# A new hand-written order for the last three units, gates and experts, and a 128-column last tile in the value product

## The chip, the core and the metric

The program runs on one core of one Trainium2 chip. Its engines work side by side and meet only at semaphores: TensorE (PE in the rows; its weight loads are PEld), VectorE (DVE), ScalarE (ACT), GpSimd (POOL) and SyncE (SP), whose queue issues nearly all transfers. The metric is the time of one execution on the device in microseconds. The kernel before took 1152.41 us, the median of three runs (1150.47 to 1155.04).

## What is computed

Two layers over x of shape (2, 1024, 256), all in float32:

```python
x = _layernorm(x + _L0_attn_ref(x, qkv, o_proj, gamma, beta))        # one head of 256, causal
x = _layernorm(x + _L0_ffn_ref(x, wq, ..., be2))
# _L0_ffn_ref:
a = _attention(_layernorm(h0, ln1_w, ln1_b), wq, bq, wk, bk, wv, bv, wo, bo)   # 16 heads of 128, rope, causal
h = h0 + a
m = _moe(_layernorm(h, ln2_w, ln2_b), w_gate, we1, be1, we2, be2)   # 4 experts of 256, the best 2 weighted
return h + m
```

Inside a head, `scores = q @ k.T`, the causal mask, a softmax over keys, `out = probs @ v`, and `out @ wo`. The mask makes every tile above the diagonal zero.

## The kernel before, in words

The attention is cut into 34 *units*, numbered by `u`: units 0 and 1 are the first layer's two batches, units 2 to 33 are the 16 heads times two batches of the second layer (`LAST` is 33). A unit has 1024 rows, eight tiles of 128 (`i`), in two chunks of 512 (`c`).

Every product is done as three matmuls, since each operand is kept as a high part and a low part in a reduced float type (`_hi`, `_lo`): high times high, high times low, low times high. That is the helper `product` (line 424 in every row). The engines share one head like this:

- PE: `project_q(u, x)` (q or k of a chunk, six matmuls 512 wide), `project_v`, `scores(u, i)`, `transposes(u, i)` of the probabilities, `outputs(u, c)` (the value product), `out_project(u, c, g)`.
- ACT: `add_bias`, `exponent`, and the high parts: `high_qk`, `high_p`, `high_o`.
- DVE: `row_max` (mask and maximum), `rotate` (the cosine term of rope), the low parts `low_p`, `low_o`, and `accumulate` into `acc`.
- POOL: `turn` (the sine term of rope) and `low_qk`, the low part of q and k.
- SP: `swap`, which brings the halves of q or k to the other partitions for `turn`, and the loads.

`outputs(u, c)` accumulates over key tiles `j` into one bank of `ps_m`. For the four tiles on the diagonal it writes only the columns from `off` on:

```python
off = min(max(0, j - TC * c), 2) * P
...
last = product(out[:, off:CH], (v_hi[:, s, j, vals], v_lo[:, s, j, vals]),
               (pT_hi[:, slot, off:CH], pT_lo[:, slot, off:CH]), j == 0, j == tiles - 1)
```

So these four tiles are 512, 384, 256 and again 256 columns wide, where the last needs only 128. The 128 columns too many read zeros that POOL writes into slot 7 of `pT_hi` and `pT_lo` once, at the start.

The order of the work is written out by hand, for each engine apart, as a list of calls: `start()` for the first units, `head(u)` for units 3 to 30, and `ends()` for what is left. Nothing reorders it: an instruction that waits for its semaphore holds up all behind it on its engine. Two rules set the waits that the change touches. PE takes the two banks of `ps_m` in turn: `take_bank` waits until the reader of the bank's last but one use is done. And the transposes use the two banks of `ps_t` in turn, freed by `low_p`.

After unit 33, `ends()` runs the gates (`gate_logits`, then `gate_copy`, `gating_1` to `gating_3` on DVE) and the experts of both batches: `expert_in(b, n)`, `gelu_mid` and `high_mid` (in `middle`) on ACT, `low_mid` on POOL, `expert_out(b, n)`, and `mix_bias` and `mix` on DVE. `low_expert(m, e)` on POOL splits the expert weights, which `load_expert` brings through two staging slots; `ln_stats`, `ln_power`, `ln_apply`, `ln_transpose`, `ln_affine` and `ln_low` are the steps of a layer norm; `add_row` and `add_x1` are additions into `acc` on POOL.

Of the kernel before, what the change touches and what calls it, by code (L numbers as in the profile page):

```python
# [101 lines left out]
def build(nc, A):  # L102

    with ExitStack() as ctx:
# [2369 lines left out]
```

## Time and profile before

| | |
|---|---|
| median of three runs | 1152.41 us |
| the profiled execution | 1155.01 us, of it 1152.9 us span |
| PE / PEld busy | 1121.9 us (97%) / 1021.8 us (89%) |
| DVE / ACT / POOL busy | 866.1 (75%) / 736.6 (64%) / 637.8 (55%) |
| chain that ended last | PE 91%, DVE 5%, POOL 1%, ACT 1% |

The span runs from the first to the last instruction; the 2.1 us around it belong to the execution and not to the program. A busy PE is not a PE at its peak: a matmul is shown from its start to its modelled end, and the next one starts before that end. So the spacing of starts says what a matmul costs. "PEclk" is the granted clock of TensorE as a share of its higher level, 2.4 GHz; 0.50 is the lower one, 1.2 GHz.

### The profile page before, as it was taken

The page shows a single profiled execution, that of the slowest core. Times are in us where ns is not written, and L with a number is a line of the kernel's source. Part 1 is how long each engine was busy: PE and PEld are TensorE (multiplying, and loading weights), DVE is VectorE, ACT ScalarE, POOL GpSimd, SP SyncE. Part 2 cuts the span into 40 slices and gives each one's busy share as a digit, 9 for nine tenths or more (in the row PEclk, how much of TensorE's full clock was granted, in tenths as well). Part 3 has the DMA queues.
Part 4 walks back from the last instruction along what each step waited for, and adds up shares of the span by engine and source line. Part 5 has one row for each costly group of instructions (what it writes and reads, how often), then busy time and mean ns, then how long its engine had stood idle before and what let it go on. Part 6 is the DMA issues. An engine that isn't in the chain of part 4 may idle for free.

```text
span 1152.9 us, 20493 instructions
## 1 busy us (share of the span) xinstructions
PE 1121.9 (97%) x7154; PEld 1021.8 (89%) x7154; DVE 866.1 (75%) x2016; ACT 736.6 (64%) x1565; POOL 637.8 (55%) x511
## 2 busy tenths in 40 slices
PE   8999999999999999999999999999999999889996
PEld 7998889999999999899999999999999998777995
DVE  6766877777777777777777777777777767867698
ACT  3746766666666666666666666666666665574753
POOL 2225756555655555656555555555555556845663
PEclk9999999999999999999999999999999999899998
DMA  5002222121212121212121212121212111221001
GB/s 170 1 1 78 63 73 55 41 60 38 51 38 60 38 51 38 60 38 51 38 60 37 51 37 61 38 51 38 60 37 51 42 38 46 65 92 37 1 20 55
DMA packets 46301, 56.55 MB, mean 49 GB/s; under 512 B 5940, under 2 KB 29176, under 8 KB 46200
## 3 DMA queue, kind: packets, MB, share of 16 engines
q1 hardware_dynamic: 45368, 54.19, 18.9%
q8 instruction: 58, 0.95, 0.3%
q10 hardware_dynamic: 832, 1.05, 0.3%
q14 instruction: 43, 0.35, 0.1%
HBM read 17.47 MB, written 4.19 MB: 19 GB/s over the span
## 4 chain that ended last, share of the span: by engine, by line
PE 91%; DVE 5%; issue 1%; POOL 1%; ACT 1%; DMA 0%; SPq 0%; POOLq 0%; DVEq 0%; ACTq 0%
PE ps_m L424 56%; PE ps_s L424 22%; PE ps_t L562 11%; PE ps_m L477 1%; PE ps_t L430 1%; DVE acc L1595 1%; DVE rows L1487 0%; DVE pT_lo L1562 0%; DVE stats L1434 0%; PE ps_m L620 0%; DVE acc L1666 0%; DVE ps_s L1555 0%; DVE work L1516 0%; DMA wst<-in_L_ffn_we 0%; DVE acc L1477 0%
## 5 line engine op out<-in xcount | busy, mean ns | idle before, releaser
L2069 POOL TENSOR_TENSOR work<-work,rope 128x512 f32<-128x512 f32 x128 | 166.8, 1303 | 229.2 <-DMA work<-work 229.2
L1562 DVE TENSOR_TENSOR pT_lo<-ps_t,pT_hi 128x512 fp32r<-128x512 f32 (+3 forms) x408 | 210.5, 550 | 40.9 <-ACT pT_hi L1065 38.4
L1065 ACT ACTIVATE pT_hi<-ps_t 128x512 fp32r<-128x512 f32 (+3 forms) x408 | 183.0, 489 | 74.9 <-PE ps_t L562 74.5
L1555 DVE CUSTOM_DVE_ANT_0 ps_s<-ps_s,causal 128x128 f32<-128x128 f32 (+7 forms) x272 | 203.2, 765 | 5.9 <-PE ps_s L424 3.3
L2080 POOL TENSOR_TENSOR qk_lo<-work,qk_hi 128x512 fp32r<-128x512 f32 x128 | 163.0, 1293 | 24.9 <-ACT qk_hi L1022 24.9
L2073 POOL TENSOR_TENSOR work<-work 128x512 f32<-128x512 f32 x128 | 167.4, 1308 | 10.1
L1595 DVE SCALAR_TENSOR_TENSOR acc<-ps_m,rinv,acc 128x256 f32<-128x256 f32 x272 | 118.5, 477 | 61.2 <-PE ps_m L424 61.1
L1016 ACT ACTIVATE work<-ps_m,bqk 128x512 f32<-128x512 f32 x128 | 88.7, 693 | 114.5 <-PE ps_m L424 114.3
L424 PE MATMUL ps_s<-qk_hi 128*128 128x384 f32 (+5 forms) x384 | 140.8, 367 | 2.0 <-POOL qk_lo L2080 1.2
L1058 ACT ACTIVATE prob_b<-ps_s,nmax 128x640 f32<-128x640 f32 (+3 forms) x136 | 130.3, 958 | 19.5 <-DVE nmax L1555 16.1
L424 PE MATMUL ps_m<-pT_hi,v_hi 128*128 128x512 f32 (+2 forms) x384 | 135.2, 352 | 3.4 <-DVE pT_lo L1562 2.5
L424 PE MATMUL ps_m<-pT_lo,v_hi 128*128 128x512 f32 (+2 forms) x384 | 134.1, 349 | 0.0
L424 PE MATMUL ps_m<-pT_hi,v_lo 128*128 128x512 f32 (+2 forms) x384 | 133.9, 349 | 0.0
L424 PE MATMUL ps_s<-qk_lo,qk_hi 128*128 128x384 f32 (+5 forms) x384 | 131.8, 343 | 0.0
L424 PE MATMUL ps_s<-qk_hi,qk_lo 128*128 128x384 f32 (+5 forms) x384 | 131.1, 341 | 0.0
L1516 DVE SCALAR_TENSOR_TENSOR work<-ps_m,bqk,rope 128x512 f32<-128x512 f32 x128 | 95.4, 745 | 47.0 <-ACT work L1016 46.8
L562 PE MATMUL ps_t<-ident,prob_b 128*128 128x128 f32 x884 | 120.3, 275 | 1.6 <-DVE pT_lo L1562 1.5
L562 PEld LDWEIGHTS ps_t<-ident,prob_b 128*128 128x128 f32 x884 | 101.9, 141 | 11.4 <-issue 2.9
L1022 ACT ACTIVATE qk_hi<-work 128x512 fp32r<-128x512 f32 x128 | 79.2, 641 | 40.6 <-POOL work L2073 40.4
L424 PE MATMUL ps_m<-hT_hi,wqk_hi 128*128 128x512 f32 x256 | 103.6, 405 | 0.0
L424 PE MATMUL ps_m<-hT_hi,wqk_lo 128*128 128x512 f32 x256 | 100.8, 394 | 0.0
L424 PE MATMUL ps_m<-hT_lo,wqk_hi 128*128 128x512 f32 x256 | 100.6, 393 | 0.0
(197 smaller groups left out, 2855.2 us busy)
## 6 DMA issues: line engine op xcount, KB each, us to landing
work<-work SPq DMA_DIRECT2D x256, 128.0 KB, 2.3
acc<-in_L_attn_x SPq DMA_DIRECT2D x8, 256.0 KB, 4.4
wst<-in_L_ffn_wq SPq DMA_DIRECT2D x16, 128.0 KB, 2.5
wst<-in_L_ffn_wk SPq DMA_DIRECT2D x16, 128.0 KB, 2.4
wo_st<-in_L_ffn_wo SPq DMA_DIRECT2D x16, 128.0 KB, 2.1
wst<-in_L_ffn_wv SPq DMA_DIRECT2D x8, 256.0 KB, 3.0
x_rows<-acc SPq DMA_DIRECT2D x4, 512.0 KB, 3.5
wst<-in_L_ffn_we SPq DMA_DIRECT2D x8, 256.0 KB, 2.9
```

Of the source, the lines that this page charges most:

```text
L424: ins = pe.matmul(out, lhs[x], rhs[y], start=first and k == 0, stop=last and k == 2)
L562: last = pe.transpose(t_bank(u, i, j)[:, k * P:(k + 1) * P], probs(i)[:, part], ident[:, :])
L1016: act.activation(qb[:, x % 2, :], m_bank("q", u, x), ACT.Identity, bias=bqk[:, j, head_:head_ + 1]).then_inc(qb_done.sem, qb_done.up(u, x))
L1058: act.activation(probs(i), all_scores[:, score_range(i)], ACT.Exp, bias=nmax[:, u % 2, i:i + 1], scale=-1.0, accum_out=rsum[:, u % 2, i:i ...
L1065: act.activation(pT_hi[:, slots, cols], t_bank(u, i, j)[:, 0:size * P].rearrange("p (j q) -> p j q", q=P), ACT.Copy).then_inc(t_hi.sem, t_ ...
L1516: dve.scalar_tensor_tensor(qc[:, ring3(u, x), :], m_bank("q", u, x), bqk[:, j, head_:head_ + 1], cos_t[:, c * CH:(c + 1) * CH], ALU.add, A ...
L1555: dve.tensor_tensor_reduce(s, s, causal[:, T - (i + 1) * P:T], -1.0, ABOVE_ALL, ALU.add, ALU.min, accum_out=nmax[:, u % 2, i:i + 1]).then_ ...
L1562: dve.tensor_tensor(pT_lo[:, slots, cols], t_bank(u, i, j)[:, 0:size * P].rearrange("p (j q) -> p j q", q=P), pT_hi[:, slots, cols].bitcas ...
L1595: last = dve.scalar_tensor_tensor(acc[:, b, tile, :], src[:, t * D:(t + 1) * D], rinv[:, u % 2, tile:tile + 1], acc[:, b, tile, :], ALU.mu ...
L2069: pool.tensor_tensor(qs[:, x % 2, :], qs[:, x % 2, :], sin_t[:, c * CH:(c + 1) * CH], ALU.mult).then_inc(sin_done.sem, sin_done.up(u, x))
L2073: pool.tensor_tensor(qc[:, ring3(u, x), :], qc[:, ring3(u, x), :], qs[:, x % 2, :], ALU.add).then_inc(rope_done.sem, rope_done.up(u, x))
L2080: pool.tensor_tensor(qk_lo[:, u % 2, j, cols], qc[:, ring3(u, x), :], qk_hi[:, u % 2, j, cols].bitcast(F32), ALU.subtract).then_inc(qk_lo_ ...
```

## The change

It has two parts. In `outputs`, the last diagonal tile becomes 128 columns wide, and the two writes of zeros at the start of POOL's program go away. And in `ends()`, the calls of all five engines stand in another order; no call is added or taken away, and all arguments stay. `start()` and `head(u)` keep their order.

```diff
@@ outputs, on PE
-                    off = min(max(0, j - TC * c), 2) * P
+                    off = max(0, j - TC * c) * P
@@ start of POOL's program
-            pool.memset(beats[:, :, :, :], 0.0)
-            pool.memset(pT_hi[:, NT - 1, 2 * P:3 * P].bitcast(F32), 0.0)
-            pool.memset(pT_lo[:, NT - 1, 2 * P:3 * P].bitcast(F32), 0.0).then_inc(const_done, 1)
+            pool.memset(beats[:, :, :, :], 0.0).then_inc(const_done, 1)
@@ ends, on PE
                 out_project(LAST - 2, 0, 0)
+                scores(LAST - 2, 7)
                 out_project(LAST - 2, 0, 1)
-                scores(LAST - 2, 7)
...
+                transposes(LAST - 2, 7)
+                project_v(VALUES - 1, 3)
+                outputs(LAST - 2, 1)
                 scores(LAST - 1, 2)
-                project_v(VALUES - 1, 3)
-                transposes(LAST - 2, 7)
                 scores(LAST - 1, 3)
-                outputs(LAST - 2, 1)
...
+                out_project(LAST - 2, 1, 1)
                 transposes(LAST - 1, 3)
                 project_q(LAST, 1)
-                out_project(LAST - 2, 1, 1)
+                scores(LAST - 1, 5)
                 outputs(LAST - 1, 0)
                 scores(LAST - 1, 6)
+                transposes(LAST - 1, 4)
+                scores(LAST - 1, 7)
+                out_project(LAST - 1, 0, 0)
+                transposes(LAST - 1, 5)
                 project_q(LAST, 2)
                 project_q(LAST, 3)
-                transposes(LAST - 1, 4)
-                scores(LAST - 1, 7)
-                transposes(LAST - 1, 5)
-                out_project(LAST - 1, 0, 0)
+                transposes(LAST - 1, 6)
                 scores(LAST, 0)
                 scores(LAST, 1)
+                ln_transpose(4, 0)
                 scores(LAST, 2)
-                transposes(LAST - 1, 6)
-                ln_transpose(4, 0)
...
                 outputs(LAST, 0)
                 transposes(LAST, 4)
-                out_project(LAST, 0, 0)
                 scores(LAST, 7)
                 transposes(LAST, 5)
+                out_project(LAST, 0, 0)
+                transposes(LAST, 6)
                 out_project(LAST, 0, 1)
-                transposes(LAST, 6)
                 expert_in(0, 0)
@@ ends, on POOL, behind the experts' first pieces
                 low_mid(0, 0)
-                add_x1(0, 1)
+                low_expert(1, 2)
                 low_mid(0, 1)
                 ln_power(5, 0)
                 low_mid(0, 2)
-                low_expert(1, 2)
+                low_expert(1, 3)
                 low_mid(0, 3)
+                ln_low(4, 1)
+                ln_low(5, 0)
                 add_row(1, 1)
@@ ends, on SP
+                load_expert(2, 1)
                 swap(LAST, 0)
+                load_expert(2, 3)
+                load_expert(2, 2)
                 swap(LAST, 1)
-                load_expert(2, 1)
-                load_expert(2, 3)
                 swap(LAST, 2)
                 swap(LAST, 3)
-                load_expert(2, 2)
```

On PE, one piece of the difference shows the value product of every head, here at its chunk 0 (the names are the written bank, then the moving and the fixed operand):

```order
 L424 MATMUL ps_m<-pT_lo,v_hi 128x256
 L424 MATMUL ps_m<-pT_hi,v_lo 128x256
-L424 MATMUL ps_m<-pT_hi,v_hi 128x256
-L424 MATMUL ps_m<-pT_lo,v_hi 128x256
-L424 MATMUL ps_m<-pT_hi,v_lo 128x256
+L424 MATMUL ps_m<-pT_hi,v_hi 128x128
+L424 MATMUL ps_m<-pT_lo,v_hi 128x128
+L424 MATMUL ps_m<-pT_hi,v_lo 128x128
 L562 MATMUL ps_t<-ident,prob_b 128x128 x5
```

Three matmuls of each `outputs` call are half as wide, 64 calls in all, and transposes follow them.

On POOL, before `scores(LAST, 0)` can run, stood these rows in the kernel before (`v_lo` is `low_expert(2, .)`, L2069 and L2073 are one `turn`, L2093 `add_row`, L2036 `ln_power`, `qk_lo` `low_qk`):

```order
L2085 TENSOR_TENSOR v_lo<-wst,v_hi 128x512
L2069 TENSOR_TENSOR work<-work,rope 128x512
L2073 TENSOR_TENSOR work<-work 128x512
L2093 TENSOR_TENSOR acc<-acc,bob 128x1024
L2069 TENSOR_TENSOR work<-work,rope 128x512
L2073 TENSOR_TENSOR work<-work 128x512
L2036 TENSOR_TENSOR rstd<-var,minus_half 128x4
L2085 TENSOR_TENSOR v_lo<-wst,v_hi 128x512
L2080 TENSOR_TENSOR qk_lo<-work,qk_hi 128x512 x2
```

and now these (two lines fewer stand above them in the file, so the same operations have numbers two lower):

```order
L2034 TENSOR_TENSOR rstd<-var,minus_half 128x4
L2083 TENSOR_TENSOR v_lo<-wst,v_hi 128x512 x2
L2091 TENSOR_TENSOR acc<-acc,bob 128x1024
L2067 TENSOR_TENSOR work<-work,rope 128x512
L2071 TENSOR_TENSOR work<-work 128x512
L2067 TENSOR_TENSOR work<-work,rope 128x512
L2071 TENSOR_TENSOR work<-work 128x512
L2078 TENSOR_TENSOR qk_lo<-work,qk_hi 128x512 x2
```

The layer norm's power and the second expert piece no longer stand between `turn(LAST, 1)` and the `low_qk` that the scores wait for.

On DVE, in unit 33, behind the 16 small operations of `gating_2(0)` (which `low_o(LAST, 0)`, the row `oT_lo`, preceded) stood before:

```order
L1573 RECIPROCAL rinv<-rsum 128x4
L1562 TENSOR_TENSOR pT_lo<-ps_t,pT_hi 128x4x128
L1562 TENSOR_TENSOR pT_lo<-ps_t,pT_hi 128x128
L1595 SCALAR_TENSOR_TENSOR acc<-ps_m,rinv,acc 128x256 x2
L1555 ISA ps_s,nmax<-ps_s,causal 128x1024
L1555 ISA nmax 128x1
```

and now:

```order
L1555 ISA ps_s,nmax<-ps_s,causal 128x896
L1555 ISA nmax 128x1
L1562 TENSOR_TENSOR pT_lo<-ps_t,pT_hi 128x4x128
L1562 TENSOR_TENSOR pT_lo<-ps_t,pT_hi 128x128
L1595 SCALAR_TENSOR_TENSOR acc<-ps_m,rinv,acc 128x256 x2
L1568 TENSOR_TENSOR oT_lo<-ps_m,oT_hi 128x512
```

So `gating_2(0)` now stands ahead of `row_max(LAST, 6)`, `low_p(LAST, 4)` and `low_o(LAST, 0)`.

## Rows read from the trace of the kernel before

**Rows 1.** Busy time by stretch: us, busy and instructions by engine, clock, DMA.

```profile
core 0: us, PE busy (x) PEld busy (x) DVE busy (x) ACT busy (x) POOL busy (x), PEclk, DMA share, GB/s
300.00:600.00 300.00, 299.94 (x1907) 273.74 (x1906) 225.65 (x500) 198.64 (x435) 172.83 (x137) 1.00 0.21 50
...
946.80:996.70 49.90, 46.94 (x284) 40.80 (x282) 38.16 (x94) 30.58 (x67) 32.18 (x25) 1.00 0.21 51
996.70:1012.30 15.60, 13.81 (x71) 12.20 (x72) 12.16 (x25) 9.61 (x21) 10.67 (x9) 0.68 0.21 60
1012.30:1042.30 30.00, 25.02 (x156) 21.86 (x155) 22.24 (x68) 19.24 (x41) 17.36 (x12) 1.00 0.25 79
1042.30:1046.50 4.20, 4.17 (x12) 3.29 (x13) 3.27 (x7) 1.73 (x3) 3.80 (x4) 0.60 0.85 248
...
1054.80:1135.20 80.40, 80.40 (x522) 73.21 (x520) 66.02 (x170) 48.64 (x79) 51.70 (x38) 1.00 0.02 8
1082.40:1150.30 67.90, 59.09 (x382) 53.56 (x381) 66.26 (x167) 34.34 (x56) 37.38 (x29) 0.97 0.07 24
```

**Rows 2.** Timeline of PE in head units: start, us, instruction; wide and narrow products.

```profile
503.75 0.28 PE L424 MATMUL ps_m<-pT_hi,v_hi 128*128 128x256 f32 x1
...
504.10 0.71 PE L562 MATMUL ps_t<-ident,prob_b 128*128 128x128 f32 x5
...
512.30 0.22 PE L424 MATMUL ps_s<-qk_hi 128*128 128x128 f32 x1
512.36 0.28 PE L424 MATMUL ps_s<-qk_lo,qk_hi 128*128 128x128 f32 x1
512.48 0.28 PE L424 MATMUL ps_s<-qk_hi,qk_lo 128*128 128x128 f32 x1
512.59 0.95 PE L562 MATMUL ps_t<-ident,prob_b 128*128 128x128 f32 x7
513.30 0.36 PE L424 MATMUL ps_s<-qk_hi 128*128 128x256 f32 x1
```

**Rows 3.** The same view: seven transposes behind a wide matmul.

```profile
966.97 0.93 PE L562 MATMUL ps_t<-ident,prob_b 128*128 128x128 f32 x7
967.65 0.36 PE L424 MATMUL ps_s<-qk_hi 128*128 128x256 f32 x1
```

**Rows 4.** Timeline of PE from 955 us: rows with idle time and what ended it.

```profile
960.72 0.39 PE L424 MATMUL ps_m<-wo_hi,oT_hi 128*128 128x256 f32 x1 [0.29 <-DVE work L1516]
...
972.15 0.47 PE L424 MATMUL ps_m<-pT_hi,v_hi 128*128 128x512 f32 x1 [0.38 <-DVE pT_lo L1562]
...
985.51 0.50 PE L424 MATMUL ps_m<-pT_hi,v_hi 128*128 128x512 f32 x1 [0.86 <-DVE work L1516]
...
996.70 0.30 PE L424 MATMUL ps_s<-qk_hi 128*128 128x128 f32 x1 [1.24 <-POOL qk_lo L2080]
...
998.51 1.47 PE L562 MATMUL ps_t<-ident,prob_b 128*128 128x128 f32 x7 [0.36 <-DVE pT_lo L1562]
...
1007.09 1.97 PE L477 MATMUL ps_m<-ident,rows 128*128 128x128 f32 x8 [1.23 <-DVE logit L1601]
...
1026.90 0.35 PE L424 MATMUL ps_m<-wo_hi,oT_hi 128*128 128x256 f32 x1 [0.96 <-DVE oT_lo L1568]
...
1028.65 0.50 PE L424 MATMUL ps_s<-qk_hi 128*128 128x512 f32 x1 [0.81 <-ACT prob_b L1058]
...
1032.86 0.95 PE L562 MATMUL ps_t<-ident,prob_b 128*128 128x128 f32 x7 [1.16 <-DVE pT_lo L1562]
...
1042.33 0.47 PE L424 MATMUL ps_m<-pT_hi,v_hi 128*128 128x512 f32 x1 [2.09 <-DVE pT_lo L1562]
```

**Rows 5.** Timeline of POOL ahead of the wait at 996.70.

```profile
991.80 1.02 POOL L2036 TENSOR_TENSOR rstd<-var,minus_half 128x4 f32<-128x4 f32 x1
992.79 1.29 POOL L2085 TENSOR_TENSOR v_lo<-wst,v_hi 128x512 fp32r<-128x512 f32 x1
994.05 2.50 POOL L2080 TENSOR_TENSOR qk_lo<-work,qk_hi 128x512 fp32r<-128x512 f32 x2
```

**Rows 6.** Timeline of DVE: two `ln_apply` calls.

```profile
996.39 1.37 DVE L1487 TENSOR_SCALAR rows<-acc,mv,rstd 128x256 f32<-128x256 f32 x4
...
1001.80 5.09 DVE L1487 TENSOR_SCALAR rows<-acc,mv,rstd 128x256 f32<-128x256 f32 x4 [0.64 <-PE ps_m L477]
```

More of the change, by code:

```diff
@@ L804, in ends @@
                 transposes(LAST - 2, 0)
+                scores(LAST - 2, 5)
+                out_project(LAST - 3, 1, 0)
                 transposes(LAST - 2, 1)
                 project_q(LAST - 1, 0)
-                scores(LAST - 2, 5)
-                out_project(LAST - 3, 1, 0)
                 transposes(LAST - 2, 2)
+                out_project(LAST - 3, 1, 1)
+                transposes(LAST - 2, 3)
                 scores(LAST - 2, 6)
-                transposes(LAST - 2, 3)
-                out_project(LAST - 3, 1, 1)
                 project_q(LAST - 1, 1)
@@ L883, in ends @@
                 out_project(LAST, 1, 0)
-                out_project(LAST, 1, 1)
                 ln_transpose(5, 0)
                 expert_out(0, 1)
+                out_project(LAST, 1, 1)
                 expert_in(0, 2)
@@ L1305, in ends @@
                 high_p(LAST - 2, 6)
+                exponent(LAST - 1, 0)
                 add_bias(LAST - 1, 3)
                 high_p(LAST - 2, 7)
-                exponent(LAST - 1, 0)
                 high_qk(LAST - 1, 2)
@@ L1323, in ends @@
                 exponent(LAST - 1, 4)
+                exponent(LAST - 1, 5)
                 high_o(LAST - 1, 0)
[L1325 removed]
                 high_qk(LAST, 0)
[L1327 to L1328 removed]
                 high_p(LAST - 1, 4)
+                high_expert(2, 2)
                 exponent(LAST - 1, 6)
                 high_qk(LAST, 1)
+                high_p(LAST - 1, 5)
+                add_bias(LAST, 2)
+                exponent(LAST - 1, 7)
                 add_bias(LAST, 3)
[L1333 to L1334 removed]
                 high_p(LAST - 1, 6)
@@ L1337, in ends @@
                 high_p(LAST - 1, 7)
-                high_expert(2, 2)
                 ln_affine(4, 1)
-                high_qk(LAST, 2)
+                high_expert(2, 3)
                 exponent(LAST, 0)
@@ L1368, in ends @@
                 middle(0, 1)
+                ln_rows(5, 0)
                 high_o(LAST, 1)
-                ln_rows(5, 0)
+                high_expert(1, 3)
                 ln_affine(5, 0)
@@ L1931, in ends @@
                 ln_stats(5, 0)
+                invert(LAST, 1)
                 low_p(LAST, 7)
+                ln_apply(5, 0)
+                gating_3(0)
                 mix_bias(0, 0)
-                invert(LAST, 1)
-                ln_apply(5, 0)
                 low_o(LAST, 1)
-                mix(0, 0, 0)
-                mix(0, 0, 1)
                 accumulate(LAST, 1, 0)
@@ L1941, in ends @@
                 ln_stats(5, 1)
+                gate_copy(1, 0)
+                mix(0, 0, 0)
+                mix(0, 0, 1)
+                ln_apply(5, 1)
                 mix_bias(0, 1)
@@ L1944, in ends @@
                 mix(0, 1, 1)
-                gate_copy(1, 0)
-                ln_apply(5, 1)
                 mix_bias(0, 2)
                 mix(0, 2, 0)
-                gate_copy(1, 1)
                 mix(0, 2, 1)
                 mix_bias(0, 3)
-                gating_1(1)
                 mix(0, 3, 0)
                 mix(0, 3, 1)
-                gating_2(1)
+                ln_stats(6, 0)
+                gate_copy(1, 1)
                 mix_bias(0, 4)
+                gating_1(1)
                 mix(0, 4, 0)
@@ L1959, in ends @@
                 mix_bias(0, 5)
-                ln_stats(6, 0)
                 mix(0, 5, 0)
+                gating_2(1)
                 mix(0, 5, 1)
@@ L1974, in ends @@
                 mix_bias(1, 1)
+                mix(1, 1, 0)
                 ln_stats(6, 1)
-                mix(1, 1, 0)
+                ln_apply(6, 0)
                 mix(1, 1, 1)
@@ L1981, in ends @@
                 mix_bias(1, 3)
+                mix(1, 3, 0)
                 ln_apply(6, 1)
-                mix(1, 3, 0)
                 mix(1, 3, 1)
+                ln_stats(7, 0)
                 mix_bias(1, 4)
@@ L2182, in ends @@
                 low_qk(LAST - 1, 3)
+                ln_power(4, 0)
                 low_expert(2, 0)
+                low_expert(2, 1)
+                add_row(0, 1)
                 turn(LAST, 0)
-                add_row(0, 1)
                 turn(LAST, 1)
-                ln_power(4, 0)
-                low_expert(2, 1)
                 low_qk(LAST, 0)
@@ L2222, in ends @@
                 low_mid(0, 10)
+                ln_low(5, 1)
                 low_mid(0, 11)
+                ln_power(6, 0)
                 low_mid(0, 12)
@@ L2227, in ends @@
                 low_mid(0, 15)
-                ln_low(5, 1)
-                ln_power(6, 0)
                 low_mid(1, 0)
```

171 lines of the change are left out of this document (80 added, 91 removed).

## The prediction

> **What bounds the kernel now.** I read the busy times by stretch first, then PE's timeline, then its waits. In the head units, 300 to 600 us, PE is busy 299.94 of 300 us at full clock, and DVE, ACT and POOL have a quarter or more of their time free [rows 1]. There a matmul taken off PE is time taken off the kernel, and nothing else is. From 946.8 us on, where `ends()` begins, it is different: ten times PE stands idle for a semaphore, for 0.29, 0.38, 0.86, 1.24, 0.36, 1.23, 0.96, 0.81, 1.16 and 2.09 us, together 9.38 us [rows 4]. The clock falls twice: over 996.70 to 1012.30 the granted clock is 0.68, over 1042.30 to 1046.50 it is 0.60, between them 1.00 [rows 1]. Both stretches follow idle time of PE (1.24 and 0.36 us; 2.09 us). From 1054.8 to 1135.2, in the experts, PE is never idle (80.40 of 80.40 us), while DVE is busy 66.02, and over the last stretch, 1082.4 to 1150.3, DVE itself is busy 66.26 of 67.90 us [rows 1]. So there are three places: heads bound by PE's own work, a stretch of 100 us with holes, and experts in which PE leads and DVE is close behind.
>
> **What the narrow tile is worth.** 64 calls of `outputs` (32 units, 2 chunks) end in three matmuls of 256 columns, now of 128. The wide three take from 503.75 to 504.10, 0.35 us [rows 2]. The trace has the narrow case in the same surroundings, `scores(u, 0)`: three products of 128 columns behind a 256-wide matmul and ahead of transposes, 512.30 to 512.59, 0.29 us, at spacings of 0.06, 0.12 and 0.11. Only the first is at half the price, since its weights were loaded under the wide matmul before; the others wait for a load each. Behind them seven transposes take 0.71 us (512.59 to 513.30), and behind a wide matmul 0.68 [rows 2, 3], so 0.03 is handed on. The times are rounded to 0.01; over all 29 such triples in the head units of the same view I find 0.285 and 0.026 handed on, and over 56 wide ones 0.356, so 0.045 us a call: 64 x 0.045 = 2.9 us. Bounds: 64 x 0.01 = 0.6 us (the rounded rows at their worst) and 64 x 0.07 = 4.5 us (nothing handed on).
> The page "TensorE: Matmul & The Clock Gate" of the Trainium skill has a rule, section "Back-to-back issue gap", of N/2.4 + 2.5 ns per warm matmul; by it each narrow matmul would save 53 ns, 192 of them 10.2 us. Its section on LDWEIGHTS gives about 107 ns (an estimate from 128 columns over 1.2) for a weight load, which by itself would allow next to no saving; this case's spacings of 0.12 and 0.11 agree with that second rule.
> The two writes of zeros at the start cost nothing and free nothing: PE and POOL both wait there for transfers and for the first statistics. If that cover were gone they would be two short writes, under 0.5 us together.
>
> **What the new order is worth.** A wait costs more than its idle time. The last matmul before it is shown for 0.28 us where the next would have started after 0.12 [rows 2], so 0.16 comes on top: ten waits are 9.38 + 1.6 = 11.0 us. The lowered clock costs at most 15.6 x 0.32 = 5.0 and 4.2 x 0.40 = 1.7 us; less what PE idles inside the first anyway I take 4.4 + 1.6 = 6.0. So 17 us lie open. I followed each wait through the new lists, with the trace's durations and every engine's queue in its new order.
> At 960.72 the bank waits for `rotate`; now `scores(LAST - 2, 7)`, some 1.4 us of matmuls, stands between. Gone: 0.45. At 972.15 `outputs(LAST - 2, 1)` waits for `low_p`; now `project_v`, twelve 256-wide matmuls or 12 x 0.12 = 1.4 us, stands behind the transposes instead of a `scores` of half that. Gone: 0.54. At 985.51 `outputs(LAST - 1, 0)` takes the bank after `project_q(LAST, 1)` and waits for its `rotate`; in the new order the bank it takes is that of `out_project(LAST - 2, 1, 1)`, emptied long before. Gone: 1.02.
> At 996.70 `scores(LAST, 0)` waits for POOL's second `low_qk`. Ahead of it stand 1.02 us of `ln_power` and 1.29 of `low_expert` [rows 5], both moved forward past the two `turn`s, into time in which POOL was waiting. PE meanwhile comes later, behind two `project_q` and seven transposes. I find `low_qk` about 1 us ahead of PE. Gone: 1.40. The 0.36 at 998.51 goes too, but `ln_transpose(4, 0)` now takes the bank of `project_q(LAST, 3)` and waits for its `rotate`, about 0.65. Added: 0.15 net.
> At 1007.09 PE waits for `gate_copy`, which is queued on DVE behind `ln_apply(4, 1)`. That call takes 5.09 us where the same four operations took 1.37 a little earlier [rows 6]: each of the four ends as an operation of POOL ends, one for one, while POOL works without a pause. In the new order POOL has `ln_low(4, 0)` and `turn` at that point, again without a pause, so the call stays slow. The wait stays, and I put it at 2.0 instead of 1.23. Added: 0.8.
> The three around 1030 (0.96, 0.81, 1.16, with their 0.48: 3.4 us) lose their causes one by one: `out_project(LAST, 0, 0)` stands behind `scores(LAST, 7)` and six transposes; `exponent(LAST, 5)` stands one call further forward on ACT; but `gating_2(0)`, 2.7 us of small operations, has moved ahead of `row_max(LAST, 6)`, `low_p(LAST, 4)` and `low_o(LAST, 0)`, so about 1.3 stays. Gone: 2.1. At 1042.33 `outputs(LAST, 1)` waits for `low_p(LAST, 7)`, still behind `ln_stats(5, 0)`, which waits for POOL's `add_row(1, 0)`; I find 1.1 instead of 2.09. Gone: 1.0. Small new waits behind `low_p(LAST - 1, 4)` and in the experts: 0.6 added.
> Sum of the waits: 0.45 + 0.54 + 1.02 + 1.40 + 2.1 + 1.0 = 6.5 gone, 0.15 + 0.8 + 0.6 = 1.55 added, 5.0 us net. The clock: the three waits within 6 us at 1026 to 1033 did not lower it, the 2.09 did; the new order keeps one wait of that size (before `ln_transpose(4, 1)`), so I leave one fall, between the 1.6 and the 4.4 us of the two seen, at 3.0. Gone: 3.0. Bounds: none (0, both falls return) and all 6.0.
> The experts keep their length: PE has no hole there to fill. The order of weight loads changes on SP, and `swap(LAST, 1)` now stands behind two loads that wait for `low_expert`; I find both earlier than `add_bias(LAST, 1)`, so it costs nothing, with about 1 us to spare. The tail after PE's last matmul is DVE's and stays.
> Sum: 2.9 + 5.0 + 3.0 = 10.9 us. The profiled execution of before took 1155.0 us (1152.9 span and 2.1 around it), 2.6 more than the median, so 1144.1 there and 1141.5 for the median.
>
> **The rivals.** (a) *DVE takes over in the experts*, 0.14. For: DVE is busy 66.26 of the last 67.90 us [rows 1], so if PE comes 8 us sooner DVE must find the 8 us in its own idle time. Against: from 1054.8 to 1135.2 DVE idles 80.40 - 66.02 = 14.4 us, mostly waiting for a PE that would now be earlier, and `gate_copy(1, 1)` has moved behind `mix` work. If half of the order's 8.0 us is lost there: 1152.4 - 2.9 - 4.0 = 1145.5, up to 1149. (b) *The order only moves the waits*, 0.15: each removed one returns as another of its size. For: a chain across five queues, and I kept or added 4 us of waits already. Against: three of the removed are bank or queue rules that the lists settle. Then only the tile counts: 1152.4 - 2.9 = 1149.5. (c) *The narrow matmuls run at half price each*, 0.04, against spacings of 0.12 and 0.11 [rows 2]: three narrow ones would take 0.18 instead of 0.35, 64 x 0.17 = 10.9 in place of 2.9: 1152.4 - 10.9 - 8.0 = 1133.5. The page's gap rule, above, says nearly the same. (d) *Slower: POOL's queue blocks behind `low_expert(1, 3)`*, 0.07. It now stands ahead of `low_mid(0, 3)`, `ln_low(4, 1)`, `ln_low(5, 0)` and `add_row(1, 1)`, and needs `high_expert(1, 3)`, which stands on ACT behind `ln_rows(5, 0)` and `high_o(LAST, 1)`. From the end of `outputs(LAST, 1)`: two ACT operations and two of 1.3 us on POOL, some 3.8 us, against 4.5 us of PE work (`expert_out(0, 0)`, `out_project`, `ln_transpose`) before `expert_out(0, 1)` needs `low_mid(0, 3)`. The margin is 0.7 us; past it every microsecond is PE's, and `expert_in(0, 4)` stands behind `ln_low(4, 1)` as well. It makes the kernel slower only when it eats the whole 10.9 us: a block of 17 us, with the lower clock in it, gives 1158.5. (e) That the change does nothing is excluded for the tile, whose matmuls are in the program.
>
> **How the numbers follow.** The forecast has 0.60: 1141.5, with 1135 to 1147 from its own bounds (tile 0.6 to 4.5, clock 0 to 6.0, waits a few either way). What a measurement tells from no change is 0.5%, 5.8 us, so faster is below 1146.6. Of the forecast nearly all, half of (a) and (c) lie there: 0.72. Within 0.5%: (b), the rest of (a) and the forecast's edge, 0.21. Slower, above 1158.2: (d), 0.07. The range leaves out (d) and (c) and holds the others: 1135 to 1150.
>
> **What would show it.** Right: the last three matmuls of `outputs` spaced 0.06, 0.12, 0.11, and the head units ending some 2.7 us earlier; no wait before `outputs(LAST - 2, 1)`, `outputs(LAST - 1, 0)` and `scores(LAST, 0)`; a wait of 1 to 3 us before `ln_transpose(4, 1)` with `ln_apply(4, 1)` at about 5 us; one stretch of lowered clock; `outputs(LAST, 1)` starting 10 to 14 us earlier than 1042.33; PE without holes in the experts. Wrong: waits on `pT_lo` or `qk_lo` elsewhere adding to more than 6 us; two falls of the clock; holes of PE on `acc` (DVE) or `wqk_lo` (POOL) after `expert_out(0, 0)`.

## The result, and the profile of the changed kernel

The changed kernel takes 1147.95 us (median of 17 runs, 1145.97 to 1150.39) where before takes 1152.41 (17 runs). The ratio is 0.9966, interval 0.9955 to 0.9977: 3.9 us faster, between 2.6 and 5.2. The forecast was 1141.5, range 1135 to 1150, with 0.72 on a gain of more than 0.5%. The time lies inside the range, but two thirds of the gain is missing, and it falls into the class that was given 0.21. The profiled execution took 1150.01 us, 5.0 less than that of before; it lies 2.1 us above its kernel's median and that of before 2.6, so the two traces can be set side by side, with one reserve that follows below.

Busy time of each engine by stretch, in the changed kernel (columns as in [rows 1]):

```profile
core 0: us, PE busy (x) PEld busy (x) DVE busy (x) ACT busy (x) POOL busy (x), PEclk, DMA share, GB/s
300.00:600.00 300.00, 299.96 (x1915) 273.56 (x1914) 226.14 (x501) 199.03 (x436) 172.96 (x138) 1.00 0.21 50
...
997.80:1003.00 5.20, 4.68 (x17) 3.83 (x18) 4.19 (x14) 4.12 (x10) 5.04 (x5) 0.67 0.20 52
1031.61:1035.10 3.49, 3.49 (x11) 2.79 (x12) 2.38 (x8) 2.99 (x6) 2.66 (x3) 0.69 0.37 139
1046.80:1145.30 98.50, 84.98 (x546) 76.09 (x544) 91.24 (x212) 50.42 (x82) 54.42 (x40) 0.97 0.05 17
1105.60:1136.80 31.20, 26.99 (x181) 24.03 (x180) 30.74 (x69) 15.92 (x28) 17.58 (x13) 1.00 0.07 23
```

The row 1046.80:1145.30 runs from `expert_in(0, 2)` to the end of DVE's last `tail_rows`. The same stretch of the kernel before, with the same calls in it on PE (546 matmuls each):

```profile
1057.70:1150.30 92.60, 83.79 (x546) 76.18 (x544) 79.58 (x204) 50.11 (x82) 54.44 (x41) 0.97 0.05 18
```

This pair holds the result. `expert_in(0, 2)` starts at 1046.8 where it started at 1057.7, 10.9 us earlier; the forecast's sum is 10.9. Then the stretch behind it takes 98.5 us instead of 92.6, 5.9 more, and 5.0 are left. PE's work there is the same, and so is POOL's (54.4). DVE is busy 11.7 us longer. Over 1105.6 to 1136.8, up to PE's last matmul, DVE has 0.5 us free of 31.2 and PE is idle 4.2. Over its own last 31.2 us (1111.8 to 1143.0) PE of before was idle 1.5, beside a DVE that was as full (30.82 us busy).

The reserve is the clock. In the traces of two other kernels of the experiments below, the calls up to `expert_in(0, 2)` stand in the order of before. One of them ("before, biases in PSUM") has the tile of before too, so up to there it is, but for two copies on ACT, the kernel before in another execution. It needs 924.8 us from PE's first value product to `expert_in(0, 2)` (127.08 to 1051.87), where the profiled execution of before needed 929.3 (128.39 to 1057.69) and that of the changed kernel 918.5 (128.33 to 1046.81). PE's idle time ahead of `expert_in(0, 2)` in the last units is nearly the same in both (10.2 us before, 9.9 in the other); the granted clock, the last number but two of a row, is not. Before:

```profile
1000.00:1020.00 20.00, 18.57 (x106) 16.83 (x106) 12.21 (x26) 12.82 (x28) 11.68 (x10) 0.77 0.17 53
1040.00:1060.00 20.00, 17.40 (x105) 15.24 (x104) 12.71 (x32) 7.79 (x14) 11.07 (x8) 0.91 0.18 54
```

and the other execution of the same calls:

```profile
1000.00:1020.00 20.00, 18.97 (x120) 17.28 (x119) 13.57 (x32) 13.54 (x31) 11.64 (x11) 0.91 0.18 56
1040.00:1060.00 20.00, 19.49 (x129) 17.60 (x128) 13.11 (x36) 10.47 (x19) 11.07 (x8) 1.00 0.12 41
```

Measured against that one, PE of the changed kernel gains 6.3 us and not 10.8. The timed executions of before spread in the same way: of the 59 beside the experiments, the 25 with a mean granted clock of 0.995 or 0.996 took 1148.9 to 1151.6 us, the 11 with 0.988 or 0.989 took 1154.5 to 1155.5. So one trace can't give the gain ahead of the experts to the tenth. What doesn't depend on this is the stretch from `expert_in(0, 2)` on: it is 92.6 us in the traces of before and of the narrow tile alone, and 98.5 in those of the changed kernel and of the new order alone. With the 3.9 us measured at the end, a typical execution must then gain about 10 us ahead of it (an estimate: 3.9 + 5.9).

The chain that ended last says it in one line. Before, it was PE 91% and DVE 5%; now:

```profile
PE 87%; DVE 8%; issue 2%; POOL 2%; DMA 1%; ACT 1%; POOLq 0%; SPq 0%; DVEq 0%; ACTq 0%
```

PE's timeline in the changed kernel: the narrow products in a head, then every row from 967 us on that the view shows with more than 0.3 us of idle time:

```profile
304.51 0.22 PE L424 MATMUL ps_m<-pT_hi,v_hi 128*128 128x128 f32 x1
304.57 0.28 PE L424 MATMUL ps_m<-pT_lo,v_hi 128*128 128x128 f32 x1
304.68 0.28 PE L424 MATMUL ps_m<-pT_hi,v_lo 128*128 128x128 f32 x1
304.80 0.73 PE L562 MATMUL ps_t<-ident,prob_b 128*128 128x128 f32 x5
...
992.78 0.66 PE L477 MATMUL ps_m<-ident,rows 128*128 128x128 f32 x4 [0.33 <-DVE work L1516]
...
998.19 1.90 PE L477 MATMUL ps_m<-ident,rows 128*128 128x128 f32 x8 [0.75 <-DVE logit L1601]
...
1019.43 0.36 PE L424 MATMUL ps_m<-wo_hi,oT_hi 128*128 128x256 f32 x1 [0.73 <-DVE oT_lo L1568]
...
1031.61 0.47 PE L424 MATMUL ps_m<-pT_hi,v_hi 128*128 128x512 f32 x1 [2.63 <-DVE pT_lo L1562]
...
1042.73 0.66 PE L477 MATMUL ps_m<-ident,rows 128*128 128x128 f32 x4 [0.63 <-DVE acc L1595]
...
1053.74 0.50 PE L424 MATMUL ps_m<-hT_hi,qk_hi 128*128 128x512 f32 x1 [0.81 <-DVE logit L1601]
...
1109.15 0.36 PE L424 MATMUL ps_s<-v_hi,qk_hi 128*128 128x256 f32 x1 [0.45 <-DVE acc L1666]
...
1111.90 0.38 PE L424 MATMUL ps_s<-v_hi,qk_hi 128*128 128x256 f32 x1 [1.09 <-DVE acc L1666]
...
1116.89 0.50 PE L424 MATMUL ps_m<-hT_hi,qk_hi 128*128 128x512 f32 x1 [0.56 <-ACT work L1088]
...
1123.70 0.36 PE L424 MATMUL ps_s<-v_hi,qk_hi 128*128 128x256 f32 x1 [0.86 <-DVE acc L1666]
...
1133.62 0.38 PE L424 MATMUL ps_s<-v_hi,qk_hi 128*128 128x256 f32 x1 [1.21 <-POOL qk_lo L2105]
```

The three narrow products start 0.06, 0.11 and 0.12 apart. Of the ten waits of [rows 4], those at 960.72, 972.15, 985.51 and 996.70 have no row any more. The one before `outputs(LAST, 1)` is larger (2.63 for 2.09). And in the experts there is a kind of row that before did not have: `expert_out` waiting for `acc L1666`, that is, for DVE's `mix` to empty a bank of `ps_s`. DVE now holds PE up.

What DVE does there, in its timeline from the second bias addition on (L1656 is `mix_bias`, four operations; L1666 is `mix`, four here for two calls):

```profile
1055.28 1.67 DVE L1656 SCALAR_TENSOR_TENSOR acc<-work,comb,acc 128x256 f32<-128x256 f32 x4
1056.99 1.66 DVE L1666 SCALAR_TENSOR_TENSOR acc<-ps_s,comb,acc 128x256 f32<-128x256 f32 x4
1058.68 6.38 DVE L1656 SCALAR_TENSOR_TENSOR acc<-work,comb,acc 128x256 f32<-128x256 f32 x4
1065.10 1.66 DVE L1666 SCALAR_TENSOR_TENSOR acc<-ps_s,comb,acc 128x256 f32<-128x256 f32 x4
1066.80 1.67 DVE L1656 SCALAR_TENSOR_TENSOR acc<-work,comb,acc 128x256 f32<-128x256 f32 x4
```

and POOL's timeline over the same time:

```profile
1053.69 1.02 POOL L2034 TENSOR_TENSOR rstd<-var,minus_half 128x4 f32<-128x4 f32 x1
1056.72 2.65 POOL L2105 TENSOR_TENSOR qk_lo<-work,qk_hi 128x512 fp32r<-128x512 f32 x2 [2.01 <-ACT qk_hi L1100]
1059.33 2.57 POOL L2099 TENSOR_TENSOR acc<-acc,rope 128x1024 f32<-128x1024 f32 x1
1061.87 2.92 POOL L2105 TENSOR_TENSOR wqk_lo<-work,wqk_hi 128x512 fp32r<-128x512 f32 x2
```

The same four operations take 1.67 us while POOL rests and 6.38 while it works through `low_mid` and `add_x1`; one by one they end 0.28 us behind the end of one POOL operation each. `mix`, which has one of its operands in a PSUM bank, takes 1.66 beside a working POOL (from 1056.99) and beside an idle one. Over all 64 bias operations, the grouped view of DVE from 1030 us on has for the kernel before

```profile
L1656 DVE SCALAR_TENSOR_TENSOR acc<-work,comb,acc 128x256 f32<-128x256 f32 x64 | 37.6, 646 | 0.3
L1666 DVE SCALAR_TENSOR_TENSOR acc<-ps_s,comb,acc 128x256 f32<-128x256 f32 x64 | 26.8, 475 | 4.6 <-PE ps_s L424 4.3
```

and for the changed one

```profile
L1656 DVE SCALAR_TENSOR_TENSOR acc<-work,comb,acc 128x256 f32<-128x256 f32 x64 | 48.7, 821 | 0.5
L1666 DVE SCALAR_TENSOR_TENSOR acc<-ps_s,comb,acc 128x256 f32<-128x256 f32 x64 | 26.9, 477 | 0.5
```

The columns behind the bar are the busy sum in us, the mean of one in ns, and the idle time before them. Undisturbed, 64 of them are 16 x 1.67 = 26.7 us. So before paid 10.9 us of waiting for POOL inside these calls, and the changed kernel pays 22.0, 11.1 more. (The 11.7 us by which DVE is busier from `expert_in(0, 2)` on have other parts too, which nearly cancel: eight operations more fall into the stretch, 3.7 us, and `nmr`, a small operation of the layer norm that also waited for POOL, takes 3.1 us less in all.) Before still had idle time in which to pay: from `ln_stats(5, 1)` on, DVE was busy 80.48 of 93.5 us. Now it is busy 90.36 of 94.9, and from 1083.3 on 60.29 of 62.0.

The page "SBUF — State Buffer" of the Trainium skill, section "Who interferes with whom", has this rule: a DVE instruction with two SBUF inputs contends with a GpSimd instruction that reads SBUF. The trace agrees: `mix_bias` (`be2` in `work` and `acc`) waits, `mix` (one input in PSUM) does not.

### The profile page after: what moved, and what is told of

Same layout as the page of the kernel before. It is cut to its first block, busy times and chain, and to the rows that moved or that the text cites. A ratio compares the mean times of both kernels' runs of the same rounds, so it can differ in the third digit from the quotient of the medians.

```text
span 1147.9 us, 20491 instructions
## 1 busy us (share of the span) xinstructions
PE 1116.9 (97%) x7154; PEld 1016.3 (89%) x7154; DVE 870.6 (76%) x2016; ACT 737.3 (64%) x1565; POOL 637.7 (56%) x509
## 4 chain that ended last, share of the span: by engine, by line
PE 87%; DVE 8%; issue 2%; POOL 2%; DMA 1%; ACT 1%; POOLq 0%; SPq 0%; DVEq 0%; ACTq 0%
PE ps_m L424 54%; PE ps_s L424 20%; PE ps_t L562 11%; DVE acc L1656 2%; DVE acc L1666 1%; DVE stats L1434 1%; DMA rope<-x_rows 1%; POOL acc L2091 1%; PE ps_t L430 1%; PE ps_m L477 1%; DVE rows L1487 0%; DVE acc L1595 0%; PE ps_m L620 0%; DVE acc L1477 0%; DVE pT_lo L1562 0%
## 5 line engine op out<-in xcount | busy, mean ns | idle before, releaser
L424 PE MATMUL ps_m<-pT_hi,v_hi 128*128 128x512 f32 (+3 forms) x384 | 131.1, 341 | 2.7 <-DVE pT_lo L1562 2.6
L424 PE MATMUL ps_m<-pT_lo,v_hi 128*128 128x512 f32 (+3 forms) x384 | 133.3, 347 | 0.0
L424 PE MATMUL ps_m<-pT_hi,v_lo 128*128 128x512 f32 (+3 forms) x384 | 133.3, 347 | 0.0
```

What stands on the lines that cost most here:

```text
L424: ins = pe.matmul(out, lhs[x], rhs[y], start=first and k == 0, stop=last and k == 2)
```

## The experiments

Two theories at the start. **Theory 1:** what PE gains ahead of the experts is lost because DVE has no room in them, its bias additions waiting for POOL. **Theory 2:** the new order of the experts' calls loses it. Twelve more kernels were run beside the kernel before. Over the three sets of runs its median was 1152.9, 1151.0 and 1151.1 us, so the ratio is the better number to compare across sets.

| kernel | median us | ratio to before, interval | start of `ln_stats(5, 1)` | from it to the end | `mix_bias` in all |
|---|---|---|---|---|---|
| before | 1152.41 | | 1056.79 | 93.5 | 37.6 |
| changed | 1147.95 | 0.9966 (0.9955 to 0.9977) | 1050.45 | 94.8 | 48.7 |
| tile alone | 1149.02 | 0.9976 (0.9963 to 0.9990) | 1049.50 | 93.5 | 37.6 |
| order alone | 1149.66 | 0.9979 (0.9965 to 0.9992) | 1050.96 | 94.9 | 48.7 |
| old experts' order | 1148.60 | 0.9978 (0.9964 to 0.9992) | 1046.27 | 96.8 | 38.0 |
| the same, repaired | 1143.25 | 0.9921 (0.9898 to 0.9945) | 1050.11 | 90.3 | 43.0 |
| `low_p` first | 1145.17 | 0.9938 (0.9915 to 0.9961) | 1045.65 | 94.8 | 48.7 |
| `out_project` back | 1145.95 | 0.9954 (0.9938 to 0.9970) | 1046.55 | 94.3 | 48.7 |
| changed, biases in PSUM | 1139.10 | 0.9892 (0.9872 to 0.9912) | 1047.74 | 86.9 | 26.6 |
| before, biases in PSUM | 1149.69 | 0.9977 (0.9959 to 0.9994) | 1050.96 | 90.3 | 26.6 |
| old experts' order, PSUM | 1139.69 | 0.9897 (0.9881 to 0.9914) | 1048.85 | 87.6 | 26.5 |
| `low_p` first, PSUM | 1137.12 | 0.9866 (0.9842 to 0.9891) | 1046.09 | 86.9 | 26.6 |
| old experts' order and `low_p` first, PSUM | 1138.16 | 0.9883 (0.9864 to 0.9903) | 1045.68 | 87.6 | 26.5 |
| the same with `out_project` back | 1137.75 | 0.9879 (0.9859 to 0.9899) | 1044.92 | 87.6 | 26.5 |

The last three columns are from the profiled execution, in us. Executions differ by 1 to 2 us before the first value product (it starts at 126.9 to 128.4 us) and by some 4 us more by the clock, as shown above, so the column of starts compares only that loosely (tile alone starts 7.3 us earlier than before, where its median is 3.4 us lower); "from it to the end" goes to the end of DVE's last `tail_rows` and does not have that error.

**The tile alone.**

```diff
-                    off = min(max(0, j - TC * c), 2) * P
+                    off = max(0, j - TC * c) * P
```

> The kernel before with the narrow tile alone (and without the two writes of zeros); its order is untouched. The changed kernel's trace gives 0.043 us a call at chunk 0 and 0.049 at chunk 1 (28 calls each), 64 x 0.046 = 2.9 us, and the whole rest of the program would only start earlier. Both theories below: 1152.4 - 2.9 = 1149.5 us, 0.25% faster. Rival: the DVE that is busy without a pause over the last 68 us of before swallows it, then 1152 us.

Measured 0.9976, 2.8 us (1.2 to 4.3). The trace behind `ln_stats(5, 1)` is that of before to a hundredth (93.50 us against 93.49): everything starts earlier together, DVE too. What comes off the heads arrives in full at the end.

**The order alone** (the changed kernel with `off` and the two writes of zeros as before).

> The changed kernel with the 256-column tile back (and the two writes of zeros): the new order alone. If tile and order add up, 1148.0 + 2.9 = 1150.9 us, so the order is worth 1.5 us and not 8. If the two get in each other's way in the experts (DVE full anyway), it comes out as the changed kernel, 1148 us.

Measured 0.9979: 2.4 us (0.9 to 4.0). With the tile's 2.8 this makes 5.2, and the two together measured 3.9 (2.6 to 5.2). They add up within what can be told. The order, forecast at 8.0 with the clock, gives about a third of it. Its stretch from `expert_in(0, 2)` on is 98.5 us for 92.6, so its 2.4 us are, by an estimate from these numbers, 8.3 gained ahead of the experts and 5.9 lost in them.

**The experts in the old order.** From `expert_in(0, 2)` on, all engines' calls as before; the list in front stays the changed one. On DVE, among others:

```diff
-                gate_copy(1, 0)
                 mix(0, 0, 0)
                 mix(0, 0, 1)
-                ln_apply(5, 1)
                 mix_bias(0, 1)
                 mix(0, 1, 0)
                 mix(0, 1, 1)
+                gate_copy(1, 0)
+                ln_apply(5, 1)
                 mix_bias(0, 2)
```

> The changed kernel, but from expert_in(0, 2) on (on DVE from ln_stats(5, 1)) the calls stand in the order of before. Theory 1: the 11.6 us that PE has gained at expert_out(0, 1) are lost to a DVE that has no room in the experts, whatever their order, since its mix_bias calls wait for POOL's operations (37.6 us for 16 calls before, 48.7 after): then about 1148 us, within 2. Theory 2: the new order of the experts itself loses them (gating and layer norm stand elsewhere on DVE and ACT): then 1148.0 less most of the 6.6 us lost, 1142 us.

Measured 0.9978. It looked like theory 1, but PE had a hole of its own in it. PE's timeline:

```profile
1054.98 0.79 PE L424 MATMUL ps_m<-hT_hi,qk_hi 128*128 128x512 f32 x1 [6.24 <-DVE logit L1601]
```

`gate_copy(1, 0)` stood too far back on DVE for the earlier PE. So the run decides nothing, and it was repeated with the two calls where the changed kernel has them.

> The run with the old order of the experts again, with one repair: there DVE's gate_copy(1, 0) stood behind mix_bias(0, 1), and PE waited 6.24 us for it at 1054.98 (the end was not later for it). Now gate_copy(1, 0) and ln_apply(5, 1) stand as in the changed kernel, the rest of the experts as before. Theory 1 (no room on DVE whatever the order): 1147 to 1149 us, though PE gets 7 us back. Theory 2 (the order of the experts): 1142 us.

Measured 0.9921, 1143.25 us: theory 2's number. The old order of the experts, with this one repair, is 4.7 us faster than the new one (1147.95 - 1143.25; 5.2 by the ratios). Its trace has 43.0 us of `mix_bias` against 48.7, and 90.3 us from `ln_stats(5, 1)` on against 94.8. So theory 1 as I had put it, "whatever their order", is wrong. Whether the order costs by itself or only through the bias calls is what the next runs tell.

**The biases in PSUM.** After the last transposes the two banks of `ps_t` are free, and `be2` (four times 256 columns) just fits. ACT copies it there behind `high_expert(1, 3)`:

```diff
+            def bias_bank():
+                act.wait_ge(be2_ld, 16)
+                act.wait_ge(t_lo.sem, t_lo.at(LAST, NT - 1, 1))
+                act.activation(ps_t[:, 0, :], work[:, 4, :], ACT.Copy)
+                act.activation(ps_t[:, 1, :], work[:, 5, :], ACT.Copy).then_inc(be2_ps, 1)
...
+                if b == 0 and u == 1:
+                    dve.wait_ge(be2_ps, 1)
+                bias = be2[:, e, :] if b == 0 and u == 0 else ps_t[:, e // 2, e % 2 * D:(e % 2 + 1) * D]
...
-                    last = dve.scalar_tensor_tensor(acc[:, b, tile, :], be2[:, e, :], comb[:, b, tile, e:e + 1],
+                    last = dve.scalar_tensor_tensor(acc[:, b, tile, :], bias, comb[:, b, tile, e:e + 1],
```

> The changed kernel with the expert biases be2 copied once by ACT into the two banks of ps_t, which are free after the last transposes, and read there by mix_bias from its second call on. Nothing else moves. Theory 1 (mix_bias waits for POOL because it reads and writes SBUF alone; mix, which reads a PSUM bank, took 0.86 to 0.88 in every call): each mix_bias falls to about 1.67, 22 us less of DVE in the experts, PE sets the end again, and its 5.5 us of waits from 1105 to 1133 and about 1 us of the tail go: 1141 us. Theory 2 (the order): the stall stays, 1147 to 1148 us.

Measured 1139.10 us, 0.9892: 8.9 us under the changed kernel, and more than expected. DVE's timeline at the place of the 6.38 us (L1667 is `mix_bias`, L1677 `mix`):

```profile
1054.34 1.66 DVE L1677 SCALAR_TENSOR_TENSOR acc<-ps_s,comb,acc 128x256 f32<-128x256 f32 x4
1056.04 1.66 DVE L1667 SCALAR_TENSOR_TENSOR acc<-ps_t,comb,acc 128x256 f32<-128x256 f32 x4
1057.74 1.66 DVE L1677 SCALAR_TENSOR_TENSOR acc<-ps_s,comb,acc 128x256 f32<-128x256 f32 x4
1059.43 1.66 DVE L1667 SCALAR_TENSOR_TENSOR acc<-ps_t,comb,acc 128x256 f32<-128x256 f32 x4
```

with POOL at work beside it:

```profile
1054.01 2.56 POOL L2116 TENSOR_TENSOR qk_lo<-work,qk_hi 128x512 fp32r<-128x512 f32 x2 [2.01 <-ACT qk_hi L1101]
1056.50 2.42 POOL L2110 TENSOR_TENSOR acc<-acc,rope 128x1024 f32<-128x1024 f32 x1
1059.09 2.56 POOL L2116 TENSOR_TENSOR wqk_lo<-work,wqk_hi 128x512 fp32r<-128x512 f32 x2 [0.16 <-ACT wqk_hi L1101]
```

But for two copies on ACT, only the place of one operand has changed, and all 16 calls take 1.65 to 1.67 us. POOL gains too: its second pair takes 2.56 where it took 2.92. The row of the 60 operations, from the grouped view:

```profile
L1667 DVE SCALAR_TENSOR_TENSOR acc<-ps_t,comb,acc 128x256 f32<-128x256 f32 x60 | 24.9, 477 | 0.4
```

The chain that ended last is PE's again:

```profile
PE 92%; DVE 4%; POOL 1%; issue 1%; DMA 1%; ACT 0%; POOLq 0%; SPq 0%; DVEq 0%; ACTq 0%
```

The same edit in the kernel before (its order, its tile):

> The kernel before (its order, its wide tile) with the biases read from ps_t, as in the run that brought the changed kernel to 1139.1 us. If the change's worth was there and DVE's waits for POOL swallowed it, then without these waits the two kernels must lie apart by what was forecast, 10.9 us: PE of before had only 1.9 us of waits behind the first expert and 1 us of tail to give back, so 1150 us against 1139.1. Rival: the biases are worth as much in either order (13.8 us off the median of before is then nearly all of them), 1143 us.

Measured 0.9977, 1149.69 us. The edit is worth 2.6 us there (0.23%, between 0.7 and 4.7 us) and 8.9 in the changed kernel. Without the waits for POOL the two kernels lie 1149.69 - 1139.10 = 10.6 us apart (0.85% by the ratios, 9.8 us, with about 3 us either way from the two intervals). The 10.9 that were forecast for the change lie well inside that.

And the old order of the experts together with the biases in PSUM:

> The changed kernel with the old order of the experts (with the repair), and with the biases in ps_t. With the biases in SBUF the old order of the experts was 4.7 us faster than the new one (1143.3 against 1148.0). If that came through the bias calls and a full DVE alone, the two orders are now the same within 1 us: 1138 to 1139.5 against 1139.1. If the new order of the experts costs something by itself, it is still 3 us or more faster: under 1136 us.

Measured 0.9897 against 0.9892: no difference. The 4.7 us between the two orders of the experts are there with the biases in SBUF and gone without. The order costs nothing by itself that these runs can tell (about 3 us either way); it sets how many bias operations fall beside a working POOL, and how long DVE has nothing left to pay with. So both theories held a part: the loss is in the bias calls, and the new order makes it larger.

**Two calls on the way into the experts.** `ln_stats(5, 1)` starts DVE's last stretch, in which the changed kernel has one pause above 0.3 us, 2.38 us at 1083.32 for the gates' exponent on ACT. First, on DVE:

```diff
+                low_p(LAST, 7)
                 ln_stats(5, 0)
                 invert(LAST, 1)
-                low_p(LAST, 7)
```

> The changed kernel with low_p(LAST, 7) on DVE ahead of ln_stats(5, 0), which waits for POOL's add_row(1, 0): outputs(LAST, 1), which idled 2.63 us for it at 1031.61, then waits about 0.4, and the lowered clock behind it (1.4 us) may go too. PE is 2.2 to 3.7 us earlier there. If DVE's chain from ln_stats(5, 1) on decides, it starts earlier by the same and the end follows unless its bias calls wait longer for POOL again: 1145 us if it follows, 1148 if the gain is swallowed as the change's was.

> The same edit on top of the biases in ps_t. PE sets the end there nearly everywhere, so the 2.2 to 3.7 us of PE come through: 1139.1 - 3 = 1136 us. If it comes through here and not in the run beside it, the loss is in the bias calls.

Measured 0.9938, 2.8 us under the changed kernel, and 0.9866, 2.0 under the one with the biases in PSUM. The wait before `outputs(LAST, 1)` falls from 2.63 to 1.41 us, with the biases in PSUM from 2.44 to 1.04, and is then ACT's (`work L1088`, the bank of `expert_in(0, 0)`), so it was smaller than expected. PE's timeline of the first:

```profile
1028.35 0.50 PE L424 MATMUL ps_m<-pT_hi,v_hi 128*128 128x512 f32 x1 [1.41 <-ACT work L1088]
```

The gain was not swallowed: the stretch from `ln_stats(5, 1)` on is 94.84 us for 94.81 without the edit, and it starts earlier. The expectation (swallowed in one, not in the other) did not come true. What the pair shows is this: with the calls behind it in the same order, DVE's stretch keeps its length, and the end moves with its start.

Second, on PE:

```diff
                 out_project(LAST, 1, 0)
+                out_project(LAST, 1, 1)
                 ln_transpose(5, 0)
                 expert_out(0, 1)
-                out_project(LAST, 1, 1)
```

> The changed kernel with one PE call put back where it stood before: out_project(LAST, 1, 1) directly behind out_project(LAST, 1, 0), ahead of ln_transpose(5, 0) and expert_out(0, 1), 4.6 us of PE. The profiles so far say that the end lies a nearly fixed 93.5 to 94.9 us behind the start of ln_stats(5, 1) (before, narrow tile alone, order alone, changed, low_p first), which waits for this call through accumulate(LAST, 1, 1) and add_row(1, 1). If that is the path, ln_stats(5, 1) starts 3.5 to 4.5 us earlier, the 1.2 us that PE waits at expert_in(0, 3) go too, and the kernel takes 1144 us. If PE's own sum decides, the moved call changes nothing: 1148 us.

Measured 0.9954, 1145.95: 1.4 us by the ratio, 2.0 by the medians, half of what was expected; the intervals of the two kernels overlap. DVE's `accumulate(LAST, 1, 1)` is 7.9 us earlier (it starts at 1039.17 where it started at 1047.08), but the POOL call behind it is queued. POOL's timeline:

```profile
1038.32 2.50 POOL L2049 TENSOR_TENSOR hT_lo<-hf,hT_hi 128x512 fp32r<-128x512 f32 x2
1041.53 2.64 POOL L2049 TENSOR_TENSOR hT_lo<-hf,hT_hi 128x512 fp32r<-128x512 f32 x2 [0.70 <-ACT hT_hi L973]
1044.13 2.39 POOL L2091 TENSOR_TENSOR acc<-acc,bob 128x1024 f32<-128x1024 f32 x1
```

`add_row(1, 1)` (L2091) now waits behind `ln_low(5, 0)` and not for PE. From the start of `outputs(LAST, 1)` to that of `ln_stats(5, 1)` it is 16.8 us instead of 18.8.

**All together.** The biases in PSUM, the old experts' order and `low_p` first, and the same with `out_project` back:

> The last one with low_p(LAST, 7) ahead of ln_stats(5, 0) on DVE. By the sum of the parts: 1139 less the 2.0 us that this edit gave with the biases in ps_t: 1137 us.

> The one before with out_project(LAST, 1, 1) put back as well. With the biases in ps_t the DVE chain is short (86.9 us) and PE sets most of the end, so an earlier ln_stats(5, 1) should give only the 1.2 to 1.8 us that PE waits for gate_copy(1, 0) behind it, less the 0.9 us of waits that stood beside this call before: 1136 to 1137 us.

Measured 1138.16 and 1137.75 us, about 1 us over what was expected, and not to be told from `low_p` first with the biases in PSUM and the new order (1137.12, 0.9866). That is the best version here: 15.4 us (12.6 to 18.2) under the kernel before.

## Why the prediction was wrong

The mechanism of the gain was right, and its sum is borne out within about 3 us; the step that failed is the one behind it.

- **The narrow tile, 2.9 us.** Right. The spacings are those read from `scores(u, 0)`. In the trace the 28 heads' calls of chunk 0 save 0.043 us each and those of chunk 1 0.049, and alone it measured 2.8 us. The 10.2 us by the formula of the Trainium skill's page "TensorE: Matmul & The Clock Gate", section "Back-to-back issue gap", did not come. The section itself gives that formula for an isolated matmul and says that it counts too little at small N, where the weight load adds to it; so the prediction asked of it more than it states. The two writes of zeros cost nothing that shows.
- **The waits and the clock, 8.0 us.** In the two profiled executions the sum was right at the place where it was formed: PE is 2.5 us earlier at the start of `ends()` (946.84 to 944.34) and 10.9 at `expert_in(0, 2)`, so 8.4 in between, some 0.3 of it the last narrow calls. That it fits to the tenth is luck: against the other execution of before's calls it is 4.5 us less. The 8.3 us worked out from the run with the order alone are the better evidence. The terms were less exact. Gone as forecast: the four at 960.72, 972.15, 985.51 and 996.70. Around 1030, 0.9 us of idle time is left of 2.9, better than forecast. Before `ln_transpose(4, 1)` 0.75 is left, not 2.0. Before `outputs(LAST, 1)` it is 2.63, not 1.1: `low_p(LAST, 7)` stands behind `ln_stats(5, 0)`, which started 3.3 us ahead of the matmul, since POOL's `add_row(1, 0)` had three calls ahead of it that waited for `add_x1`'s transfer. I had this wait's chain right and its lateness wrong. The clock fell twice and not once, to 0.67 over 5.2 us and to 0.69 over 3.5, at most 2.8 us together, where 3.0 were left for one fall. The prediction also took the two falls of its one trace of before as fixed, and other executions of the same calls have a smaller one or none at these places.
- **"The experts keep their length: PE has no hole there to fill."** This is the step that failed. They became 5.9 us longer. That PE had no hole said only that DVE was fast enough for a PE that came late. I had the row that spoke against it (DVE busy 66.26 of the last 67.90 us [rows 1]) and answered it with DVE's 14.4 us of idle time before. That answer took the length of DVE's calls as fixed. They were not: 8 of the 16 `mix_bias` calls of before took from 1.9 to 5.7 us instead of 1.67, 10.9 us of waiting for POOL in all. I had read this very pattern in `ln_apply(4, 1)` [rows 6] and used it only there.
- **Rival (a)**, DVE takes over, was the right one, with 1145.5 to 1149 for it and 1147.95 measured. Half of the order's gain was put as lost, and 5.9 of 8.0 was; its chance of 0.14 was the mistake.
- **Rival (b)** is wrong: the waits were not moved but removed. **(c)** is wrong. **(d)** did not come: `low_mid(0, 3)` ended at 1041.80 and `expert_out(0, 1)` started at 1043.14 without a wait.
- **Where the 5.9 us went**, by PE's own timeline: 1.2 at `expert_in(0, 3)`, which waits for `gate_copy(1, 0)` behind `ln_stats(5, 1)` on DVE; about 5.5 from 1105 on, for `mix` and what hangs on it, where before lost 2.0; and 1.2 in the tail behind PE's last matmul. Seen from DVE, `ln_stats(5, 1)` starts only 6.3 us earlier (1056.79 to 1050.45) where PE has gained 10.9, and the stretch behind it is 1.3 us longer: `out_project(LAST, 1, 1)` now stands behind `expert_out(0, 1)` on PE, and `ln_low` ahead of `add_row(1, 1)` on POOL. The prediction did not follow this path; putting the PE call back gave 1.4 to 2.0 us. The experiments give the cause of nearly all of the 5.9: with the biases in PSUM the kernel is 8.9 us faster, and the 4.7 us between the two orders of the experts are gone.

What stays open: why in each order just so many bias calls fall beside POOL's work. It was followed call by call in the traces (10 slow calls of 16 now, 8 before), but no run set by itself which bias calls meet POOL's work. It is also open how often each of before's falls of the clock comes, since there is one trace of it.

## What to carry to other kernels

Before crediting a gain on the leading engine, look at the next engine over the stretch behind it, and look at its calls one by one: if the same call has two durations, part of its busy time is waiting, and its idle time is not room that can be spent. Where such a wait is between DVE and POOL, moving one operand into a free PSUM bank can be worth more than any order; here 8.9 us for a few lines. And find the call from which an engine runs to the end almost without pauses: as long as the calls behind it keep their order and their length, the program's end moves with the start of that call (94.8 us behind `ln_stats(5, 1)` in the changed kernel and with `low_p` first, but 90.3 with the old experts' order). Last, one trace is one execution: before a fall of the clock is counted as time to be won, look whether the executions of the same kernel all have it.
